# The second attention's output: identity and bias products against accumulating transfers

## The reference, cut to what matters

```python
    xn = _layernorm(x, axis=-1)
    x = x + _L1_attn_ref(xn, ..., L1_attn_Wout, L1_attn_bout) + _L1_ffn_ref(xn, ..., L1_ffn_b2)
...
    # _L1_attn_ref, last line
    return jnp.einsum('bld,ed->ble', y, Wout) + bout
...
    # _L1_ffn_ref: per token, the two best of 8 experts, gates = softmax of their two logits
        out_i = h @ w2[i] + b2[i]
        gate_i = jnp.sum(gates * (sel == i), axis=-1, keepdims=True)
        return acc + out_i * gate_i
```

## Time and profile before

| | |
|---|---|
| median of 3 runs | 1643.01 us (1640.13 to 1647.08) |
| the profiled execution | 1642.2 us from first to last instruction |
| mean granted TensorE clock | 0.981 |
| busy share of TensorE | 94% (1543.8 us) |
| busy share of VectorE / ScalarE / GpSimd | 53% / 45% / 44% |

### The profile page before, as it was taken

How to read it: one execution, slowest core, us unless ns; L and a number is a source line. 1 busy time by engine, 2 the same in 40 slices (tenths; PEclk the granted TensorE clock), 3 DMA queues, 4 the chain that set the end, 5 groups by cost and what they waited for, 6 DMA issues and landing times.

```text
span 1642.2 us, 32345 instructions
## 1 busy us (share of the span) xinstructions
PE 1543.8 (94%) x10802; PEld 1184.8 (72%) x10802; DVE 865.9 (53%) x2424; ACT 733.1 (45%) x1923; POOL 717.8 (44%) x815
## 2 busy tenths in 40 slices
PE   6989989999989999999997799998999999999997
PEld 3545445555547999998665467767999899999996
DVE  6777897887822444442577778874222122222220
ACT  4544545565551323323656566644333343334332
POOL 3122235666532555553810467763333433333332
PEclk9999999999999999999998999999999999999999
DMA  8533325445305343444631385367333333333331
GB/s 271 128 113 93 89 79 99 93 103 99 87 4 237 106 114 111 114 115 120 207 103 65 103 222 104 79 102 293 58 54 53 51 57 53 55 59 58 53 55 23
DMA packets 154639, 167.60 MB, mean 102 GB/s; under 512 B 84820, under 2 KB 132816, under 8 KB 151408
## 3 DMA queue, kind: packets, MB, share of 16 engines
q1 hardware_dynamic: 129936, 128.15, 30.8%
q0 software_dynamic: 24544, 37.38, 10.5%
HBM read 104.10 MB, written 44.45 MB: 90 GB/s over the span
## 4 chain that ended last, share of the span: by engine, by line
PE 68%; DVE 9%; issue 8%; POOL 8%; DMA 3%; ACT 3%; SPq 1%; DVEq 0%; POOLq 0%; ACTq 0%
PE PS L1660 23%; PE PS L1678 22%; POOL SLOT L954 6%; PE PS L1517 4%; DVE PS L1980 3%; PE PS L1453 3%; PE PS L1502 3%; PE PS L1481 2%; PE PS L1463 2%; PE PS L1543 2%; PE PS L1634 2%; PE PS L1588 2%; POOL arena L1056 1%; POOL arena L1062 1%; ACT arena L1178 1%
## 5 line engine op out<-in xcount | busy, mean ns | idle before, releaser
L1660 PEld LDWEIGHTS PS<-arena 128*128 128x128 f32 x3408 | 398.3, 193 | 16.2 <-DVE arena L2201 4.9
L1660 PE MATMUL PS<-arena 128*128 128x128 f32 x3408 | 405.3, 276 | 3.5 <-DVE arena L2201 3.5
L1678 PE MATMUL PS<-arena 128*128 x1704 | 392.3, 379 | 0.0
L1678 PEld LDWEIGHTS PS<-arena 128*128 128x128 f32 x1704 | 312.4, 190 | 39.7 <-issue 0.2
L1980 DVE CUSTOM_DVE_ANT_0 PS<-PS,arena 128x512 f32<-128x512 f32 (+3 forms) x512 | 235.4, 523 | 46.0 <-PE PS L1481 41.9
L995 POOL DMA_INDIRECT out<-arena x71 | 111.6, 1573 | 296.4 <-ACT arena L1272 274.6
L1262 ACT ACTIVATE arena<-PS,arena 128x128 f32<-128x128 f32 x568 | 161.8, 368 | 138.3 <-PE PS L1660 135.9
L2226 DVE COPY arena<-arena 128x8 f32 x71 | 12.5, 175 | 348.3 <-ACT arena L1262 326.9
L928 POOL TENSOR_SCALAR_AFFINE_SELECT arena<-arena 128x256 f32<-128x256 f32 x256 | 99.5, 412 | 206.5 <-ACT arena L1178 206.1
L981 POOL DMA_INDIRECT arena<-XN,arena x142 | 145.8, 1027 | 100.4 <-PE PS L1645 40.6
L1178 ACT ACTIVATE arena<-PS 128x512 f32<-128x512 f32 (+1 forms) x256 | 166.3, 705 | 49.5 <-PE PS L1502 39.2
(11 more groups left out here) (248 smaller groups left out, 2031.4 us busy)
## 6 DMA issues: line engine op xcount, KB each, us to landing
arena<-FD SPq DMA_DIRECT2D x32, 512.0 KB
arena<-in_w SPq DMA_DIRECT2D x16, 1024.0 KB
SPL<-arena SPq DMA_DIRECT2D x32, 384.0 KB, 2.6
arena<-SPL SPq DMA_DIRECT2D x64, 192.0 KB
XN<-arena SPq DMA_DIRECT2D x16, 512.0 KB, 3.0
arena<-SPL SPq DMA_DIRECT2D x64, 128.0 KB
arena<-SUM SPq DMA_DIRECT2D x16, 512.0 KB, 6.8
arena<-in_x SPq DMA_DIRECT2D x8, 512.0 KB, 6.8
```

What stands on the lines that cost most here:

```text
L1660: ins = pe.matmul(o, m.now[i % 2][:, c * F + 128 * f:c * F + 128 * f + 128], m.xt[i % 2][:, 128 * c:128 * c + 128], start=(c == 0), stop=( ...
L1678: ins = pe.matmul(to, m.hT[i % len(m.hT)][:, 128 * c:128 * c + 128], m.WD[:, bass.ds(e * (nf * 256) + c * 256, 256)], start=(c == 0), stop ...
```

## The change

- `project_out` keeps only the two products with `Wout`. The identity product, the bias product, and GpSimd's preparation of the bias parts (`bias_split`) are gone.
- The rows of `ACC` are stored to the output in the third stage: behind each store to `XN`, SP issues a second one of the same 512 KB to the output. The four `store_sums` are gone.
- `out_copy` now puts the bare attention output in `ACC`, and GpSimd adds it to the stored rows: one accumulating transfer of 128 x 256 values per tile (`add_sums`), at the end of the next turn's steps. The experts' first accumulation waits for all 32.
- The bias is added to the second bias of all experts (`bias_rows`), which reaches each token with weights that sum to one.

```diff
@@ second_order
-        if n % 8 == 1 and n > 8:
-            out.append(("store_sums", n // 8 - 1))
+        if n > 0:
+            out.append(("add_sums", n - 1))
...
-    out += [("rows",)] + [(kind, NT - 1) for kind in ("update", "sums_copy", "project_out", "out_copy")]
+    out += [("rows",)] + [(kind, NT - 1) for kind in ("update", "sums_copy", "project_out", "out_copy", "add_sums")]
@@ sync
-            def store_sums(c):
-                sp.wait_ge(oe_put, 8 * c + 8)
-                sp.dma_start(ov[c], ACC.rearrange("p (b i) d -> p i b d", b=NB)[:, c]).then_inc(sums_out, 16)
...
                     sp.dma_start(xnd[b], xn1[b % 2]).then_inc(xn_out[b % 2], 16)
+                    sp.dma_start(ov[b], ACC[:, 4 * b:4 * b + 4, :]).then_inc(rows_out, 16)
@@ gpsimd
             def bias_rows():
                 pool.memset(B2S, 0.0).then_inc(b_cut)
-                pool.wait_ge(b_in, 32)
+                pool.wait_ge(b_in, 48)
+                pool.tensor_tensor(bstage[0:8, :], bstage[0:8, :], bo8[0:8, :], ALU.add).then_inc(b_cut)
...
-                    pool.wait_ge(sums_out, 64)
+                    pool.wait_ge(sums_out, 16 * NT)
...
-            def bias_split():
...
+            def add_sums(n):
+                i = ORDER1[n]
+                pool.wait_ge(oe_put, n + 1)
+                pool.dma_start(out[128 * i:128 * i + 128, :], ACC[:, i, :], accum_op=ALU.add).then_inc(sums_out, 16)
@@ scalar
             def project_out(n):
                 act.wait_ge(out_made, n + 1)
+                if n == 0:
+                    act.wait_ge(rows_out, 16 * NB)
                 act.activation(ACC[:, ORDER1[n], :], ps(1, 256, 512), ACT.Copy).then_inc(oe_put)
@@ tensor
-                pe.matmul(ps(1, 256, 512), ident, ACC[:, ORDER1[n], :], start=True, stop=False)
                 pe.wait_ge(yt_put, n + 1)
                 for g in range(2):
-                    pe.matmul(ps(1, 256, 512), YT[:, 128 * g:128 * g + 128], WOUT[:, g, :], start=False, stop=False)
-                pe.matmul(ps(1, 256, 512), ones3[0:96, :], BO3[0:96, :], start=False, stop=True).then_inc(out_made)
+                    ins = pe.matmul(ps(1, 256, 512), YT[:, 128 * g:128 * g + 128], WOUT[:, g, :], start=(g == 0), stop=(g == 1))
+                ins.then_inc(out_made)
```

More of the change, by code:

```diff
@@ L400, in build @@
         b1row = view(base + 640, 128)
+        bo8 = view(base + 768, 256)
         tiles4 = lambda v: v.rearrange("p (i d) -> p i d", i=4)
@@ L437, in build @@
         RB = view(carve(8), 8)
-        BO = view(carve(256), 256)
         LREG = top[0]
@@ L624, in build @@
         kd_put, y_made, yt_put, dm_made, m_put = (sem(n) for n in ("kd_put", "y_made", "yt_put", "dm_made", "m_put"))
-        out_made, oe_put, sums_out = (sem(n) for n in ("out_made", "oe_put", "sums_out"))
+        out_made, oe_put, rows_out, sums_out = (sem(n) for n in ("out_made", "oe_put", "rows_out", "sums_out"))
         xt_ready = {b: [(banks0[f"xt{c}", b][0], banks0[f"xt{c}", b][1] + 1) for c in range(2)] for b in range(NB)}
@@ L767, in sync @@
                     slots(0)
-            sp.wait_ge(b_cut, 6)
+            sp.wait_ge(b_cut, 7)
             for k in range(3):
@@ L828, in sync @@
             early = list(EARLY)
-            ov = out[0:T, :].rearrange("(b i p) d -> i p b d", b=NB, p=128)
-            def store_sums(c):
-                sp.wait_ge(oe_put, 8 * c + 8)
-                sp.dma_start(ov[c], ACC.rearrange("p (b i) d -> p i b d", b=NB)[:, c]).then_inc(sums_out, 16)
+            ov = out[0:T, :].rearrange("(b i p) d -> b p i d", b=NB, p=128)
             for kind, *a in plan2:
@@ L853, in sync @@
                     slots(1)
-                elif kind == "store_sums":
-                    store_sums(*a)
                 elif kind == "decay_load":
@@ L869, in sync @@
             second_over(sp)
-            store_sums(3)
             for q in range(8):
@@ L935, in bias_rows @@
                 pool.memset(B2S, 0.0).then_inc(b_cut)
-                pool.wait_ge(b_in, 32)
+                pool.wait_ge(b_in, 48)
+                pool.tensor_tensor(bstage[0:8, :], bstage[0:8, :], bo8[0:8, :], ALU.add).then_inc(b_cut)
                 for k in range(3):
-                    if k:
-                        pool.wait_ge(b_cut, 2 * k + 1)
+                    pool.wait_ge(b_cut, 2 * k + 2)
                     pool.tensor_copy(b3[0:8, k, :], bstage[0:8, :]).then_inc(b_cut)
                     if k < 2:
-                        pool.wait_ge(b_cut, 2 * k + 2)
+                        pool.wait_ge(b_cut, 2 * k + 3)
                         pool.tensor_tensor(bstage[0:8, :], bstage[0:8, :], b3[0:8, k, :], ALU.subtract).then_inc(b_cut)
@@ L1016, in weights @@
             def weights():
-                pool.wait_ge(l1_in, 160)
+                pool.wait_ge(l1_in, 144)
                 for c in range(2):
@@ L1086, in gpsimd @@
                     sums(*a)
+                elif kind == "add_sums":
+                    add_sums(*a)
                 elif kind == "weights":
@@ L1092, in gpsimd @@
                     const1()
-                    bias_split()
                 elif kind == "gates" and a[1] == 4:
```

38 lines of the change are left out of this document (9 added, 29 removed).

## The result

The changed kernel takes 1668.45 us (median of four runs, 1666.02 to 1674.73); the kernel before took 1643.30 in the same comparison (1640.13 to 1647.08). The ratio is 1.0155, with a 95% interval of 1.0131 to 1.0180: slower, by 1.6%. The profiled execution has a span of 1664.3 us, 22.1 more than the 1642.2 of before.

What follows compares the result with a forecast made beforehand. TensorE was taken to set the pace, GpSimd close behind and setting it after the change. Terms 17 + 1 - 1 - 0.5 = 16.5 us on 1642.2, plus 0.8, gave 1659.5, said as 1659; own range 1652 to 1667, outer 1639 to 1673.

Steps and rivals of the forecast that it cites:

- three signs of being wrong: Accumulating rows under 0.6 us, `open` still waiting for VectorE, or GpSimd waiting for `out_copy` turn after turn.
- TensorE sets the pace: Second attention: TensorE bounds the 7.05 us turn; without the removed products its turn could fall to 6.07 us.
- The 1.3 us of turn 31: Turn 31, where only TensorE works: removed products take 1.3 us off its path.
- One accumulating transfer, A = 1.57: GpSimd's add in 24 turns: 1.57 us each plus 0.30 of issue, 44.9 us in all.
- A = 0.99: Lower cost of GpSimd's added transfer: the last scatter comes 11 us later in place of 17.
- The scan in such a turn: With TensorE waiting for `open`, scatters or `open` meet VectorE's scan: 5 us over 24 turns, 2 of them taken.
- The added wait: GpSimd's `add_sums` waits for `out_copy` ahead of scatters and `open`: counted at nothing, up to 1.3 us a turn.
- The cover: The awaited `out_copy` hangs on the previous turn's `open`, a whole turn of GpSimd's work earlier, so no wait is counted.
- The stores, +1: Third stage, eight stores of 512 KB: the one ahead of the decays costs 1 us, at worst 2.5.
- The end, -0.5: After the last scatter: later gathers cost 0.5 us beyond turn 31's saving, an earlier decay load saves 1.
- A transfer cheaper than 0.6 us: Rival on GpSimd's added transfer: at A = 0.43 the kernel takes 1633 us, a gain; chance 0.07.
- The clock: Rival: TensorE idles in turns set by GpSimd and its clock falls, 12 us more, 1671; chance 0.12.

Runs made afterwards that it cites:

- e2: Changed kernel without the adds of the stored rows, output rows stored by SyncE four times: 1647.61 us, ratio 1.0008 to the kernel before.
- e3: Changed kernel with none, one, two or three scatters a turn, the other 28 behind turn 30: turns of 6.7 to 7.1, 7.05, 7.03 to 7.19, 7.3 to 8.4 us.
- e8: Changed kernel with GpSimd products, then three plain transfers, then three scatters a turn: TensorE's product 0.07, 0.06 to 0.08, 0.55 to 1.79 us late.
- e10: Changed kernel with six plain transfers of the scatters' size in each of turns 6 to 17: product 0.06 to 0.08 us late there.
- e5: Changed kernel with each add a turn later and behind the turn's scatters, the last two behind the gathers: 1647.64 us, ratio 1.0034 to the kernel before.
- e1: Changed kernel with each add a turn later, still ahead of the scatters, the last two behind the gathers: 1658.86 us, ratio 1.0074 to the kernel before.
- e4: Changed kernel with four accumulating transfers of eight tiles in place of 32 of one: 1670.68 us, ratio 1.0131 to the kernel before.

## Why the prediction was right in its time and wrong in its reasons

The time was forecast as 1659 us, slower by 16; it came out at 1668, on the forecast side and inside the outer range of 1639 to 1673, but 1.5 us above the forecast's own range of 1652 to 1667 (whose lower end should be 1653.5 by its own terms). The last scatter's stretch was to grow by 17 us and grew by 16.7. That agreement is luck: the steps that led there were not what happened, and errors of both signs cancelled. Of the three signs of being wrong that the prediction named, one came true and one in part: GpSimd waits for `out_copy` turn after turn, and `open` still waits for VectorE, 9.8 us in place of 29.4.

*"TensorE sets the pace", a turn of 6.07 us possible.* The step that failed first. The products' worth was counted at nothing because GpSimd could not keep up; e2 says that it is nothing even without any added work on GpSimd, since TensorE waits 1.40 us for `weigh` in every turn whether or not something fills it. I read full occupancy as the bound. The start of `project_val` 0.15 us after the end of `weigh` would have shown that two things end together there. The 1.3 us of turn 31 fit e2, whose end takes 22.5 us against 23.8.

*One accumulating transfer, A = 1.57.* Mis-sized: 0.97 us in these turns, near the lower of the two GpSimd rows that I had (0.99), though it accumulates. The term was 44.9 us of GpSimd's time and is some 24 x 1.27 = 30.5. By the prediction's own working at A = 0.99 the last scatter would be 11 us later, 9.6 of them for scatters that run into the scan (next step).

*The scan in such a turn.* It didn't come about. It took TensorE to wait for `open`, and TensorE waits 0.4 us ahead of those transposes in the whole stretch, not almost 2 us a turn. With GpSimd waiting for `out_copy` behind `open`, the scatters come after the scan, at 1.03 us each.

*The added wait, counted at nothing.* It fell as the prediction said it might: GpSimd waits for `out_copy` turn after turn, 36.9 us in the stretch. The cover ("a whole turn of GpSimd's work earlier") was wrong, because `out_copy` doesn't hang on the last `open` alone but, through the held product, on the last scatters. Yet the wait itself isn't the price: in e3 GpSimd waits 1.0 to 1.5 us in turns that stay at 7.05. What costs is where the wait puts the scatters, beside TensorE's narrow products (of 32 rows or columns), and no step of the prediction had that: ten turns with a late product hold 11.7 of the 15.3 us of the sixteen turns. The late product was in the rows, though: at 935.36 and 944.99 in the trace of before, where three scatters follow each other without the scan between them, ScalarE's copy is 2.9 and 3.2 us late. The second of these:

```profile
941.16 0.62 PE L1853 MATMUL PS<-arena 128*32 128x128 f32 x16
...
943.33 0.96 POOL L954 DMA_INDIRECT SLOT<-arena  x1 [0.30 <-issue]
...
944.99 0.38 ACT L1347 ACTIVATE arena<-PS 128x256 f32<-128x256 f32 x1 [3.34 <-remote]
```

I had read VectorE's hold on the scatters as a cost only; in the kernel before it also kept the scatters away from TensorE's products.

*The stores, +1.* About right. From the store of the first decays to the load behind it takes 4.44 to 4.50 us in every kernel with the new stores and 3.81 in the two without, so a store ahead costs some 0.7 us there; it is lost in the spread of the first `open` (860.2 to 867.8).

*The end, -0.5.* Mis-sized by 8 us. The gathers' start was worked out nearly right (7.4 us after the table's turn, measured 9.0); that their rows then need 4.3 us until TensorE can transpose them, that the add of tile 31 would stand among them (2.05 us), and that TensorE's clock would fall while it waits was not.

*The rivals.* A transfer cheaper than 0.6 us: no. The clock: in 1000 to 1050 the granted clock was 0.97 against 1.00 before, and single stretches later fell lower (0.67 in 1078 to 1082, 0.57 in 1110 to 1114); in those two `project_qk` takes 2.75 and 2.88 us in the chain in place of 1.72. Three turns without a late product are long by it: 8.59, 8.28 and 8.28 us (granted clock 0.76 in 1013 to 1020, 1077 to 1084 and 1108 to 1115) against 7.05 and, in the last turns, 6.59. That is some 5 of the 22 us; in 1000 to 1050 TensorE is busy 44.4 us of 50, where it was 50.0. So this rival came true in part, with TensorE's idle time coming from the late products and not from `open`.

What stays open is why an indirect transfer holds TensorE's products. The runs show that neither GpSimd's occupation (e8) nor plain transfers of the same size (e10) nor accumulating ones of 1 KB rows (e5) do it, and that the hold ends 0.4 to 0.8 us after the row of the last scatter. The Trainium skill ("Perfetto Trace Analysis", section "DMA Instruction — SWDGE (GPSIMD)") says that such a row ends when the last descriptor is written, not when the data has moved. The last scatter of the kernel before agrees: its row lasts 0.96 us and it lands after 5.75. That would let the hold last beyond the row, into the scatter's writes; but it ends well before such a landing, and no run here shows the single writes. Whether the product itself, the signal of its end or TensorE's next instruction is held, the rows don't tell apart, since they model the ends of products. Nor was it tried whether wide products would be held as the narrow ones (32 rows or columns) are; the wide ones that happen to lie beside a first scatter, as L1748 in the changed kernel, were followed by VectorE 0.11 us after their row's end.

## What to carry to other kernels

An engine that is busy without a gap need not be the bound: look at whether its next instruction starts when its own last one ends or when another engine's does, and whether the work that you want to remove lies inside such a wait. An operation that is added to an engine's fixed order costs less by its length than by what it pushes where; the same 32 transfers cost 25 us in one place and 6 in another. When an experiment takes a wait away, read what waits afterwards before its time is taken as the price of that wait: in e1 another wait of 16.8 us had come in its place. And in front of a serial end, put what the next stage waits for ahead of what only has to be done some time.

## What the runs showed of the hardware that was not expected

- Indirect transfers of GpSimd hold TensorE's narrow products (32 rows or columns) that lie beside them: 0.2 us with one, 1.2 to 1.8 us in turns where three follow each other 0.30 us apart (e3), up to 3.2 in the kernel before.
- GpSimd's price for a transfer without an index list: 0.59 us for 128 rows of 8 bytes (six in 3.52 us at 993.80 in e10; the single rows overlap and last 0.85 on the mean), 0.97 for 128 accumulated rows of 1 KB, 1.7 for 1024 of them (e4). The Trainium skill gives 0.62 us for a transfer of GpSimd's alone ("SBUF — State Buffer", section "A bandwidth-pool intuition that's wrong"); the first of these is near it, the others are not.
